# A last stage written out by hand for every engine, with output banks by batch and head, its own MLP buffers and split shares

## What is computed

```python
q, k = rope(xn @ Wq.T), rope(xn @ Wk.T)            # 16 heads of 128
v = xn @ Wv.T ; g = xn @ Wg.T
s = clip(xn @ Ws1.T @ Ws2.T + bs2, -32, 32)        # 64 slots a head
z = cumlogsumexp(s, time) ; es = exp(s) ; enz = exp(-z)
A = tril(q @ k.T * scale)
qv = softmax(enz * (A @ es))
W2 = tril((qv * enz) @ es.T)
o = W2 @ v
o_g = o * rsqrt(mean(o * o) + eps) * g_norm * silu(g)
attn = o_g @ Wo.T
mlp = (gelu(xn @ Wgate.T) * (xn @ Wup.T)) @ Wdown.T
out = x + attn + mlp
```

## Time and profile before

| | |
|---|---|
| median of 3 runs | 1106.58 us (1105.44 to 1108.48) |
| the profiled execution | 1107.82 us |
| its span, first to last instruction | 1105.5 us |
| TensorE (PE) busy | 1079.0 us, 98% |
| VectorE (DVE) busy | 893.4 us, 81% |
| ScalarE (ACT) busy | 658.5 us, 60% |
| GpSimd (POOL) busy | 418.3 us, 38% |
| chain that ended last | PE 92%, DVE 4%, ACT 2% |
| mean granted TensorE clock | 0.989 |

### The profile page before, as it was taken

The page is one execution under the profiler, slowest core; times in us unless marked ns, Lnnn a source line. Parts: engine busy times, 40 slices in busy tenths (PEclk is TensorE's granted clock), DMA queues, the critical chain, the costliest instruction groups (busy, mean ns, idle before and its releaser), DMA issues.

```text
span 1105.5 us, 20596 instructions
## 1 busy us (share of the span) xinstructions
PE 1079.0 (98%) x7176; PEld 931.0 (84%) x7176; DVE 893.4 (81%) x1681; ACT 658.5 (60%) x2111; POOL 418.3 (38%) x308
## 2 busy tenths in 40 slices
PE   8899999999999999999999999999999999999986
PEld 7688888888888888888888888888888888888875
DVE  7887888888878887788887887888887888778763
ACT  5566565566655576655666656566665557565541
POOL 7253252433523364332634325243352336423131
PEclk9899999999999999999999999999999999999996
DMA  5020000200002000020000200020000200000001
GB/s 168 1 72 9 1 1 1 77 3 1 1 1 79 1 2 1 2 78 2 1 2 2 78 1 1 1 73 7 1 1 1 79 1 1 1 1 20 9 13 38
DMA packets 9527, 23.06 MB, mean 21 GB/s; under 512 B 849, under 2 KB 5841, under 8 KB 8529
## 3 DMA queue, kind: packets, MB, share of 16 engines
q1 hardware_dynamic: 9424, 21.76, 5.7%
HBM read 19.66 MB, written 2.10 MB: 20 GB/s over the span
## 4 chain that ended last, share of the span: by engine, by line
PE 92%; DVE 4%; ACT 2%; issue 1%; POOL 1%; DMA 0%; POOLq 0%; DVEq 0%; ACTq 0%
PE bank L209 22%; PE bank L211 20%; PE bank L210 20%; PE bank L370 5%; PE bank L307 5%; PE bank L341 3%; PE bank L320 3%; PE bank L309 2%; PE bank L379 2%; PE bank L363 1%; PE bank L332 1%; PE bank L536 1%; PE bank L350 1%; PE bank L323 1%; PE bank L297 1%
## 5 line engine op out<-in xcount | busy, mean ns | idle before, releaser
L1233 POOL TENSOR_TENSOR inter_lo<-ffb,inter_hi 128x512 fp32r<-128x512 f32 x64 | 81.5, 1296 | 501.4 <-ACT inter_hi L685 501.4
L1224 POOL TENSOR_TENSOR qkT<-ra,xs 128x512 f32<-128x512 f32 x128 | 164.9, 1288 | 104.4 <-DVE xs L951 82.1
L647 ACT ACTIVATE sm<-bank,mx 128x64 f32<-128x64 f32 x256 | 76.5, 326 | 143.3 <-DVE mx L907 143.3
L948 DVE TENSOR_TENSOR ra<-bank,rope 128x512 f32<-128x512 f32 x128 | 88.0, 688 | 57.5 <-ACT xs L629 55.0
L896 DVE RECIPROCAL enzT<-enzT 128x256 f32<-128x256 f32 x64 | 111.5, 1743 | 0.0
L628 ACT ACTIVATE xs<-bank 64x512 f32<-64x512 f32 x128 | 76.2, 595 | 55.6 <-PE bank L211 39.0
L951 DVE TENSOR_TENSOR xs<-xs,rope 128x512 f32<-128x512 f32 x128 | 107.0, 836 | 0.0
L209 PE MATMUL bank<-xh,wqk_hi 128*128 128x512 f32 x256 | 106.6, 416 | 0.0
L209 PE MATMUL bank<-xh,wgu_hi 128*128 128x512 f32 x256 | 105.4, 412 | 0.0
L209 PE MATMUL bank<-wvg_hi,xh 128*128 128x512 f32 x256 | 101.1, 395 | 1.0 <-DVE xl L1005 1.0
L211 PE MATMUL bank<-xh,wgu_lo 128*128 128x512 f32 x256 | 100.9, 394 | 0.0
(11 more groups left out here) (150 smaller groups left out, 3056.9 us busy)
## 6 DMA issues: line engine op xcount, KB each, us to landing
raw<-in_w_qkvg SPq DMA_DIRECT2D x7, 1024.0 KB, 7.5
scaled<-in_w_scaled SPq DMA_DIRECT2D x8, 640.0 KB, 8.6
packed<-in_w_packed SPq DMA_DIRECT2D x8, 384.0 KB, 3.2
acc<-in_x SPq DMA_DIRECT2D x4, 512.0 KB, 8.2
out<-acc SPq DMA_DIRECT2D x3, 512.0 KB, 3.0
raw<-in_w_qkvg SPq DMA_DIRECT2D x2, 512.0 KB, 6.4
out<-acc SPq DMA_DIRECT2D x2, 256.0 KB, 2.1
ws_raw<-in_w_slot SPq DMA_DIRECT2D x8, 48.0 KB, 3.0
```

The source lines that it names most:

```text
L647: ins = act.activation(sm[:, c], src[:, c], ACT.Exp, bias=mx[:, g:g + 1], accum_out=ssum[:, g:g + 1])
L948: dve.tensor_tensor(two(ra[i % 2][:, :]), two(pj[i][:, :]), cos, ALU.mult).then_inc(cos_done, 1)
L1224: pool.tensor_tensor(qkT[:, i, :], ra[i % 2][:, :], xs[i % 2][:, :], ALU.add).then_inc(roped, 1)
L1233: pool.tensor_tensor(inter[1][e][:, :], ffb[e][:, :], inter[0][e][:, :].bitcast(F32), ALU.subtract).then_inc(inter_lo, 1)
```

## The change

Every engine's loop now ends one stage earlier (stages 0 to 30 keep their lists), and the last stage is a list of its own for each engine:

- `o` of the last stage lies in four banks, one for a batch and head (`o_last`), and values, squares, norm, gate and transposes go by batch, not by head.
- The MLP's product of the last stage goes to `wqk` (`inter_last`), whose weights aren't needed any more, so that it needn't wait until `inter` has been read.
- The previous stage's shares are multiplied out in halves, MLP and attention (`previous_outputs`), into `sc[0]` and `pj[3]`, at other places of TensorE's list; `add_share` reads these banks.
- The slot reads go to `sc[0]`, the softmax transposes to `sc[1]`, the slot weights to `rg`.
- `slot_reads`, `slot_states` come before `gated_transpose`, after two MLP tiles in place of four; the MLP tiles are taken in the order 0, 2, 1, 3.
- The output's four tiles lie in `rg` and `sc[1]` (`last_out`), added in three passes (two tiles, one, one) and brought out by three transfers (256, 128 and 128 KB).

The helpers that are shared take the bank or tile as an argument; the places where the loops said `if not last` lose the condition. The core of the diff (removed lines left out, the new ones and their context kept):

```diff
...
+        LAST = STEPS - 1
+        LAST_BP = BP - 1
+        o_last = [[sc[1], pj[0]], [pj[1], pj[2]]]
+        ogT_last = [sc[0], pj[0]]
+        inter_at = [[t[:, :] for t in pair] for pair in inter]
+        inter_last = [[w[:, e, :] for e in range(2)] for w in wqk]
+        def last_out(i):
+            if i < 2:
+                return rg[0][:, i * D:(i + 1) * D]
+            return rg[1][:, 0:D] if i == 2 else sc[1][:, 0:D]
...
+            for k, (i, n) in enumerate(((0, 2), (2, 1), (3, 1))):
+                rows = slice(LAST_BP * NT + i, LAST_BP * NT + i + n)
+                sp.wait_ge(acc_done, 2 * LAST + k + 1)
                 sp.dma_start(out_rows[:, rows, :], acc[:, rows, :]).then_inc(out_sent, 16)
+            sp.wait_ge(out_sent, 16 * (BP - 1 + 3))
...
+            def previous_outputs(b, units, dst):
+                for tt in range(2):
+                    cols = slice((2 * b + tt) * P, (2 * b + tt + 1) * P)
+                    for s in units:
+                        src = ogT if s < 2 else inter
+                        mm = three(pe, dst[:, tt * D:(tt + 1) * D], [src[u][s % 2][:, cols] for u in range(2)],
+                                   [w[:, s, :] for w in wod], s == 2 and tt == 0, s == 1 and tt == 1)
+                if units == (0, 1):
+                    mm.then_inc(out_full, 1)
+            def last_carried():
+                for b, h in ((0, 0), (0, 1), (1, 0), (1, 1)):
+                    t = slice(b * T + P, (b + 1) * T)
+                    g = slice(h * M, (h + 1) * M)
+                    pe.matmul(o_last[b][h][:, DV:2 * DV], qe[g, t], state[g, b, :], start=True, stop=False)
+            def last_values(b):
+                for h in range(2):
+                    pe.wait_ge(W_diag, 2 * LAST + 1 + h)
+                    for tt in range(2):
+                        i = 2 * b + tt
+                        mm = pe.matmul(o_last[b][h][:, tt * DV:(tt + 1) * DV], Wt[h][:, i, :],
+                                       vS[LAST_BP % 2][:, i, h * DV:(h + 1) * DV], start=False, stop=tt == 1)
+                mm.then_inc(o_full, 1)
+            def last_transpose(b):
+                pe.wait_ge(og_done, 2 * LAST + b + 1)
+                for h in range(2):
+                    for tt in range(2):
+                        c = (2 * b + tt) * 256 + h * DV
+                        mm = pe.transpose(ogT_last[b][:, (2 * h + tt) * P:(2 * h + tt + 1) * P],
+                                          og[:, c:c + DV], ident[:, :])
+                mm.then_inc(ogT_full, 1)
+            def last_inter(i, start):
                 cols = slice(i * P, (i + 1) * P)
+                for s in (2, 3):
+                    three(pe, last_out(i), [inter_last[u][s % 2][:, cols] for u in range(2)],
+                          [w[:, s, :] for w in wod], start and s == 2, False)
+            def last_outputs(i, stop):
+                cols = slice(i * P, (i + 1) * P)
+                for s in (0, 1):
+                    mm = three(pe, last_out(i), [ogT[u][s][:, cols] for u in range(2)],
+                               [w[:, s, :] for w in wod], False, stop and s == 1)
+                if stop:
                     mm.then_inc(out_full, 1)
...
+            st, bp, hp = LAST, LAST_BP, HP - 1
+            for i in (0, 1):
+                pe.wait_ge(W_diag, 2 * st - 1 + i)
+                scores(st, bp, i, hp)
+            mlp_up(st, bp, hp, 0)
+            for i in (2, 3):
+                pe.wait_ge(A_off, 4 * st + i - 1)
+                scores(st, bp, i, hp)
+            mlp_up(st, bp, hp, 2)
+            slot_reads(st, sc[0])
+            slot_states(st, bp)
+            gated_transpose(st)
+            slot_rows(st)
+            mlp_up(st, bp, hp, 1)
+            mlp_up(st, bp, hp, 3)
+            pe.wait_ge(inter_lo, 2 * st)
+            previous_outputs(0, (2, 3), sc[0])
+            slot_softmax(st, sc[1])
+            pe.wait_ge(ogT_hi, 2 * st)
+            pe.wait_ge(ogT_lo, 2 * st)
+            previous_outputs(0, (0, 1), sc[0])
+            pe.wait_ge(qe_ready, st + 1)
+            slot_weights(st, bp, rg)
+            pe.wait_ge(ff_gelu, 2 * st + 2)
+            pe.wait_ge(inter_done, 2 * st + 1)
+            last_carried()
+            pe.wait_ge(inter_done, 2 * st + 2)
+            previous_outputs(1, (2, 3), pj[3])
+            last_values(0)
+            last_values(1)
+            previous_outputs(1, (0, 1), pj[3])
+            pe.wait_ge(inter_lo, 2 * STEPS)
+            last_inter(0, True)
+            last_inter(1, False)
+            last_inter(2, True)
+            last_transpose(0)
+            last_inter(3, True)
+            last_transpose(1)
+            for i in range(NT):
+                pe.wait_ge(last_hi, i // 2 + 1)
+                pe.wait_ge(last_lo, i // 2 + 1)
+                last_outputs(i, i > 0)
...
+            st = LAST
+            off_diagonal(st, 0)
+            off_diagonal(st, 1)
+            gate_square(st, 0, 0)
+            off_diagonal(st, 2)
+            off_diagonal(st, 3)
+            gate_square(st, 1, 1)
+            gate_tanh(st, 0)
+            copy_state(st)
+            gated_hi(st, 0)
+            gated_hi(st, 1)
+            softmax_exp(st)
+            gate_tanh(st, 1)
+            act.wait_ge(qk_full, 4 * STEPS)
+            hidden_hi(st, 0, inter_last[0])
+            hidden_hi(st, 1, inter_last[0])
+            for b in range(2):
+                act.wait_ge(o_full, 2 * st + b + 1)
+                if b == 0:
+                    act.wait_ge(msn_done, st)
+                for h in range(2):
+                    for tt in range(2):
+                        k = 2 * (2 * b + tt) + h
+                        ins = act.activation((osq, osq1)[h][:, (2 * b + tt) * DV:(2 * b + tt + 1) * DV],
+                                             o_last[b][h][:, tt * DV:(tt + 1) * DV], ACT.Square,
+                                             accum_out=ms[:, k:k + 1])
+                ins.then_inc(ms_done, 1)
+            for b in range(2):
+                act.wait_ge(ogT_full, 2 * st + b + 1)
+                if b == 0:
+                    act.wait_ge(out_full, 2 * st)
+                for h in range(2):
+                    ins = act.activation(ogT[0][h][:, b * T:(b + 1) * T], ogT_last[b][:, h * T:(h + 1) * T], ACT.Copy)
+                ins.then_inc(last_hi, 1)
...
+            st, par = LAST, LAST_BP % 2
+            score_diagonal(st, 0)
+            score_diagonal(st, 1)
+            norm_arg(st)
+            score_diagonal(st, 2)
+            score_diagonal(st, 3)
+            gate_scale(st)
+            gate_arg(st, 0)
+            gate_o(1 - par, 0)
+            gate_o(1 - par, 1)
+            softmax_in(st, par, sc[0])
+            gate_arg(st, 1)
+            softmax_max(st)
+            gate_gelu(st, 0)
+            gated_lo(st, 0)
+            gated_lo(st, 1)
+            hidden(st, 0, 2)
+            softmax_inverse(st)
+            slot_query(st, par, sc[1])
+            gate_gelu(st, 1)
+            hidden(st, 1, 3)
+            weight_diagonal(st, 0, rg)
+            weight_diagonal(st, 1, rg)
+            add_share(st, LAST_BP - 1, 0, sc[0])
+            last_norm(0)
             last_gate(0)
+            last_norm(1)
+            add_share(st, LAST_BP - 1, 1, pj[3])
             last_gate(1)
             last_gated_lo(0)
             last_gated_lo(1)
+            last_share(0, 0, 2, rg[0][:, :])
+            last_share(1, 2, 1, last_out(2))
+            last_share(2, 3, 1, last_out(3))
...
+            norm_pow(LAST)
+            hidden_lo(LAST, 0, inter_last)
+            hidden_lo(LAST, 1, inter_last)
+            for b in range(2):
+                c = slice(4 * b, 4 * b + 4)
+                pool.wait_ge(mse_done, STEPS + b)
+                if b == 0:
+                    pool.wait_ge(scal_done, LAST)
                 pool.tensor_tensor(rstd[:, c], mse[:, c], mhalf[:, c], ALU.pow).then_inc(pow_done, 1)
...
```

More of the change, by code:

```diff
@@ L352, in slot_states, with carried @@
                 mm.then_inc(state_full, 1)
-            def carried(st, last):
+            def carried(st):
                 wait(pe, acc_done, 2 * st)
-                if not last:
-                    pe.wait_ge(J_ready, st + 2)
+                pe.wait_ge(J_ready, st + 2)
                 for b in range(2):
@@ L469, in _, with stage @@
             slot_inner(1, sc[1])
-            def stage(hp, bp, first, last):
+            def stage(hp, bp, first):
                 st = 4 * hp + bp
@@ L1084, in stage @@
                     gated_lo(st, 0)
-                if not last:
-                    clip(st + 1, npar, sc[0][:, :])
+                clip(st + 1, npar, sc[0][:, :])
                 if not first:
@@ L1092, in stage @@
                     x_bias(prep)
[L1093 to L1099 removed]
+                gate_g(st + 1, npar, 0)
+                if first:
+                    invert(0, 0, 0)
+                else:
+                    cumulate(st + 1, npar)
+                gate_g(st + 1, npar, 1)
```

(3 more changed lines are left out.)

285 lines of the change are left out of this document (110 added, 175 removed).

## The result

| | before | after |
|---|---|---|
| median of the runs, us | 1107.46 (1105.44 to 1108.48, 4 runs) | 1091.45 (1091.29 to 1093.50, 4 runs) |
| ratio | | 0.9866, 95% interval 0.9853 to 0.9879 |
| profiled execution, its span, us | 1107.82, 1105.5 | 1093.50, 1091.5 |
| mean granted clock | 0.989 | 0.995 |

The kernel became 1.34% faster; 1091.2 was forecast. Before's median gained one run since the forecast and reads 0.9 us higher.

A forecast was written before the change was run, and what follows sets the result against it. Bound: last-stage waits uncovered by a next stage, each paid again through slow matmuls. 6.85 + 3.2 - 1.25 + 2.65 - 0.25 + 4.05 + 0.15 = 15.4 us saved, from 1106.58 to 1091.2; range 1088.5 to 1096.5.

The forecast's parts named there:

- Up to the reduction: Last stage, first scores to softmax reduction: MLP tiles and shares put behind the chain, shorter gate wait; gain 6.85 us.
- Reduction to exponentials: With MLP output in `wqk`, ScalarE has almost nothing ahead of the exponentials; 3.95 us falls to 0.7, gain 3.2.
- Exponentials to weights: Exponentials to slot weights: TensorE late by 0.9 us, not the chain; 5.4 us where it was 4.15, loss 1.25.
- Weights to squares: Slot weights to first squares: 4.1 us from 6.75, half by clock, rest by squares after one batch; gain 2.65.
- Squares to transposes: First squares to first transposes: 2.87 us from mean square to transposes, for a batch as for a head; loss 0.25.
- To the end: First transposes to last addition: 6.4 us where it was 10.45; gain 4.05, of which the clock is 2.4.
- The tail: Last addition to end of span, 2.57 us: loses perhaps 0.15, since the last transfer is half as large.
- The clock: TensorE at full clock throughout the last stage: longest idle 1.35 us, and an earlier 2.1 us wait kept full clock.
- One fall in the stage: Rival: one clock fall in the last stage, likeliest before the second transposes; 1093.6 to 1094.1 us; chance 0.23.
- Late handovers: Rival: handovers between engines late, costing 3 us, at worst with a clock fall; 1094.2 to 1097 us; chance 0.10.
- Not as it says: Rival: something other than `inter` holds ScalarE's exponentials; gain about 8 us, time 1098.5; chance 0.03.
- slower: Rival: small TensorE pieces early in the stage drop the clock for good; a fall at 1065 gives 1112 us; chance 0.02.

The follow-up runs named there:

- the kernel with all tiles first: Changed kernel with the third and fourth MLP tiles put back ahead of the slot reads; 1093.86 us, ratio 0.9885.
- the exchange of two lines: Kernel before, with ScalarE's exponentials of the last stage moved ahead of its two copies of the MLP output; 1101.67 us, ratio 0.9959.
- the weights moved ahead: Changed kernel with slot weights ahead of the second half of share 0 and values ahead of both halves of share 1; 1091.69 us, ratio 0.9860.
- the waits filled: Kernel before, order and waits kept, with identity matmuls into unused banks in TensorE's three long waits of the last stage; 1101.91 us, ratio 0.9961.
- by head: Changed kernel with values, squares, norm, gate, transposes and output matmuls of its end going by head, in the same four banks; 1091.96 us, ratio 0.9870.
- the shared buffer: Changed kernel with the last MLP product in `inter` again, ScalarE's copies waiting for the previous stage's shares; 1095.81 us, ratio 0.9901.
- the two norms: Changed kernel with both norms ahead of the first gate on VectorE and the second addition behind both gates; 1090.39 us, ratio 0.9845.

## Why the prediction was right

- **Up to the reduction** (6.85 forecast): 6.74. The tile move alone is 2.7 us of it, and 2.0 of the stage, as the kernel with all tiles first shows.
- **Reduction to exponentials** (3.2): 3.23. The cause given, the copy that waits for the shares, is shown by the exchange of two lines. The means wasn't the one named: the separate buffer frees nothing here, because ScalarE's new list has the exponentials first. What it carries are the squares, 3.4 us later without it plus a fall of the clock; the prediction didn't price that.
- **Exponentials to weights** (loss of 1.25): loss of 1.05 from the first exponential. TensorE was late, not the query, as said, but by 0.5 us and not 0.9: with the weights moved ahead they start that much earlier and wait for the query.
- **Weights to squares** (2.65): 2.62, and the reason was half wrong. It gave half to the clock and half to squares that begin after one batch. All of it is the clock: in the order of before with the waits filled the step is 4.15 us, as in the changed kernel. In before too the first squares began when half of the values were done, and by head the waves of transposes start at the same distances.
- **Squares to transposes** (loss of 0.25): loss of 0.23.
- **To the end** (4.05): 3.98, of which the clock is 2.7 in the kernel with the waits filled, 2.4 forecast. The tail, from the last addition to the end of the span, is 0.39 us shorter where 0.15 was forecast; no run takes the three output transfers alone.
- **Sum:** 15.4 forecast, 15.68 measured in the stage. The span differs by the late start of the stage, 1.68, which isn't the change's. By the medians the gain is 16.0 against the kernel before, measured beside it. The forecast of 1091.2 took a before of 1106.58, which is 0.9 lower, so part of the closeness of 1091.2 to 1091.45 is luck of that size.
- **The clock.** Full from 1057 to the end, as forecast, and no swing between the levels in a stream broken by groups, which the Trainium skill, "TensorE: Matmul & The Clock Gate", Part 1, warned of. What it says of run-to-run variation is borne out: the clock fell behind the 2.1 us wait, which I took as a sign of safety, in the very next profile. That argument of the prediction was wrong: the full clock came out as forecast, but one of its grounds doesn't hold. The 1.2 us wait that is left in the last stage was shorter, and no profile here shows a fall behind it, nor behind the 1.9 us of the kernel with all tiles first; behind the 3.3 us wait of the shared buffer there is one.
- **Rivals.** One fall in the stage: not seen in any profile of the changed kernel. Late handovers: no milestone is late by more than 0.12 us. Not as it says, slower: excluded.

## What to carry to other kernels

- In the stretch of a program where the next stage's work no longer covers waits, lay every engine's list out from measured starts and distances: nine milestones came within 0.3 us. Price each wait twice where it is long enough to drop the matmul clock, but then expect gains that remove the same fall not to add.
- Before moving work out of a chain's way, ask whether the engine then waits less in all. With the weights first TensorE waited 1.4 us in place of 1.2, only elsewhere. What helps is what lets two waits of different engines run side by side, as the two norms did.
- Exchange two lines first: 5.8 of 15.7 us came from the order in which one engine took its copies and its exponentials.

## What the hardware showed that I had not expected

- Behind a TensorE wait of 2.1 us at the same place, 25 to 28 us, the clock fell to 1.2 GHz in three of the thirteen profiles in which it was not filled, for 3.5 us in the changed kernel's. They are the three in which the wait ended latest (28.15 to 28.27 us, 27.20 to 27.74 in the rest). Behind two waits of 1.8 and 1.15 us near 50 us, with 0.66 us of work between them, it fell in all thirteen, for 3.4 us in five and 6.8 in eight. A short wait is a chance of a fall, not a safe one, and the fall's price is another matter: nothing at 28 us, 0.3 to 1.8 us near 50.
- A VectorE pass over four columns of two SBUF operands took 1.00 us in place of 0.16 while GpSimd was subtracting, and ended with it. A pass over eight columns at the beginning of the changed kernel's last stage took 0.55 us and ended within 0.02 us of a GpSimd pass, 1061.53 and 1061.51. Passes that read a PSUM bank kept their length beside GpSimd (two `weight_diagonal` passes, 1.29 us, beside a subtraction of 1.29; the reduction and the addition of the earlier trace rows, as large, take 1.29 in all with GpSimd idle).
